# Layer 3's opening made within layer 2's last graphs, and three steps of layer 0 moved, in a four-layer graph attention kernel

## The reference

```python
h = jnp.maximum(_layernorm(x, axis=-1), 0.0)
x = x + L0(h, adj, ...)   # q, k, v; per 128-column chunk a softmax of clip(qk/sqrt(32), -10, 10), masked to -10
                          # ctx @ Wo.T + bo + h, layer norm, gamma, beta
x = x + L1(relu(ln(x)))   # e = leaky(e_i + e_j), softmax over neighbours, elu
x = x + L2(relu(ln(x)))   # the same with 8 heads, a prior, and @ W_out.T at the end
# layer 3
h1, h2, h3 = h @ W1, h @ W2, h @ W3
e = leaky_relu(h1 @ h2.T, 0.2)
e = where(adj > 0, e, -1e12)
x = x + relu(softmax(e) @ h3)
```

## Time and profile before

| | |
|---|---|
| median of 3 runs | 2028.11 us (2024.01 to 2032.48) |
| profiled execution | 2026.8 us, of which span 2024.6 |
| mean granted TensorE clock | 0.911 |
| busy in the span: PE, DVE, ACT, POOL | 82%, 79%, 66%, 6% |
| 0 to 660 us (layer 0 and the way to layer 1): PE, DVE, ACT | 543.5, 546.0, 404.9 us |
| 660 to 1643 us (layers 1 and 2) | 780.4, 814.7, 756.6 us |
| 1643 to 2024.6 us (layer 3) | 326.5, 243.2, 178.1 us |

### The profile page before, as it was taken

One profiled execution on the slowest core, in us unless ns is written; L12 is line 12 of the kernel. 1 busy time (PEld: TensorE's weight loads), 2 busy tenths in 40 slices (PEclk: granted clock), 3 DMA queues, 4 the chain that ended last, 5 costly groups with the idle time before them and its releaser, 6 DMA issues. The chain is left out here.

```text
span 2024.6 us, 36872 instructions
## 1 busy us (share of the span) xinstructions
PE 1650.5 (82%) x13620; PEld 1056.3 (52%) x13620; DVE 1603.9 (79%) x2710; ACT 1339.6 (66%) x1751; POOL 126.2 (6%) x130
## 2 busy tenths in 40 slices
PE   3998988988986577999999777977797748999997
PEld 1444443434433356777777556755675534555554
DVE  4888988988987557888888889898888747666764
ACT  2766666666663576777776989888888814554553
POOL 1000010010000100000000000000000000000000
PEclk7999999999998688999999878888888869999999
DMA  8634634635622311111111112111211120000000
GB/s 232 160 102 122 141 92 115 147 89 127 141 71 68 119 43 39 47 43 42 50 46 43 54 64 74 65 64 55 74 65 64 63 89 1 11 22 10 10 11 21
DMA packets 74922, 146.49 MB, mean 72 GB/s; under 512 B 11937, under 2 KB 34722, under 8 KB 74754
## 3 DMA queue, kind: packets, MB, share of 16 engines
q1 hardware_dynamic: 74754, 144.23, 25.4%
HBM read 101.85 MB, written 8.78 MB: 55 GB/s over the span
## 5 line engine op out<-in xcount | busy, mean ns | idle before, releaser
L1097 ACT ACTIVATE g<-s_all,steep_d 128x1024 fp8e4<-128x1024 f32 x608 | 642.3, 1135 | 40.6 <-DMA s_all<-s_rows 20.6
L1032 PE MATMUL acc<-parts,g 128*128 128x102 bf16 (+1 forms) x6144 | 417.2, 229 | 24.7 <-DVE sums L1188 24.5
L1032 PEld LDWEIGHTS acc<-parts,g 128*128 128x128 fp8e4 x6144 | 401.5, 100 | 57.4 <-issue 40.5
L1014 PE MATMUL post<-parts,edge 128*128 128x396 bf16 (+1 forms) x1024 | 233.7, 384 | 88.4 <-DVE base L1196 88.4
L583 ACT ACTIVATE e<-s_ps 128x1024 f32<-128x1024 f32 x256 | 248.1, 1022 | 24.5 <-PE s_ps L439 22.3
L1181 DVE TENSOR_TENSOR g<-g,edge 128x1024 int32<-128x1024 int32 x192 | 228.1, 1220 | 34.1 <-ACT g L1097 34.1
L732 DVE SCALAR_TENSOR_TENSOR e<-e,bound 128x1024 f32<-128x1024 f32 x160 | 191.0, 1228 | 43.4 <-ACT e L583 43.3
L1014 PEld LDWEIGHTS post<-parts,edge 128*128 128x128 fp8e4 x1024 | 102.5, 102 | 195.9 <-issue 111.5
L435 PE MATMUL s_ps<-qs,ks 128*128 128x512 f32 x512 | 193.5, 487 | 6.6 <-DMA ks<-split 4.9
L451 PE MATMUL sum_ps<-e,pick 128*32 128x256 f32 x2048 | 142.2, 396 | 67.6 <-DVE e L732 57.4
L1879 ACT ACTIVATE z<-z,shift 128x1024 f32<-128x1024 f32 x64 | 73.6, 1149 | 161.0 <-DVE shift L1955 161.0
(11 more groups left out here) (158 smaller groups left out, 2146.7 us busy)
## 6 DMA issues: line engine op xcount, KB each, us to landing
s_all<-s_rows SPq DMA_DIRECT2D x96, 512.0 KB, 3.7
inv_all<-inv_rows SPq DMA_DIRECT2D x256, 128.0 KB, 2.9
qs<-split SPq DMA_DIRECT2D x128, 128.0 KB, 3.2
ks<-split SPq DMA_DIRECT2D x128, 128.0 KB, 2.8
x<-in_x SPq DMA_DIRECT2D x8, 512.0 KB, 6.8
inv_rows<-inv SPq DMA_DIRECT2D x32, 128.0 KB, 1.8
adj_in<-in_adj SPq DMA_DIRECT2D x8, 512.0 KB, 4.1
out_x<-x SPq DMA_DIRECT2D x8, 512.0 KB, 3.2
```

What stands on the lines that cost most here:

```text
L1014: ins = pe.matmul(self.post[:, it % 2, 0:H * 3 * W1].rearrange("p (h k c) -> p h k c", h=H, k=3), self.c.edge[:, jt, it * P:(it + 1) * P], ...
L1032: ins = pe.matmul(self.acc[:, bank, o:o + self.NS], self.g[:, h % RING, jt, it * P:(it + 1) * P], self.upper[par][:, jt, h, :, :].rearrang ...
L1097: act.activation(self.g[:, h % RING, jt, :], self.s_all[:, h % 2, :], ACT.Relu, bias=self.steep_d[par][:, jt, h:h + 1], scale=STEEP, satur ...
```

## The change

Layer 3's `prepare` is taken out of its block and becomes the class `Opening`, whose parts are called from `additive_layers` for layer 2's last two graphs (and, in the branch that doesn't run, from a block of its own, `open_apart`). SyncE loads the three weights and `adj` tiles 0 to 3 between the heads of graph 6 and tiles 4 to 7 after heads 4 to 7 of graph 7; the input has four buffers instead of two. VectorE takes the statistics of graph 0 in step h=0 of graph 7, tiles 0 to 3 of `bias` in h=1 to 4, tiles 4 and 5 in h=6, tiles 6 and 7 in h=7. GpSimd's rstd stands in graph 7. PE makes `w12` in h=0, the transpositions in h=2 and the projection in h=4, in layer 2's `aux`. ScalarE copies `w12` and makes `h` in h=3, copies `ht` in h=6 and `q` in h=7. `bias`, the first `ht` and the first `q` lie in `c.arena`, which is also the `parts` buffer of the even graphs.

In layer 0 PE's `output(b - 1, 1)` goes from step 11 to 10, VectorE's second `residual` from 12 to 10 and its `low` for k from 10 to 9.

```diff
--- before.py
+++ after.py
@@ -509,7 +509,7 @@
                         elif i == 8:
                             pe.wait_ge(v_ready, n + 1)
                             k(n)
-                    if i == 11 and not first:
+                    if i == 10 and not first:
                         if more:
                             pe.wait_ge(k_split, n + 1)
                         output(b - 1, 1)
@@ -807,14 +807,14 @@
                     if not first:
                         if i == 2:
                             update(b - 1, 0)
-                        elif i == 12:
+                        elif i == 10:
                             residual(b - 1, 1 - par, 1, more)
                         elif i == 14:
                             update(b - 1, 1)
                     if more:
                         if i == 5:
                             low(n, q_hi, bq, q_split, k_lo_stacked)
-                        elif i == 10:
+                        elif i == 9:
                             low(n, k_hi, bk, k_split, q_lo_stacked)
                     if not (isinstance(b, int) and b >= B - 2):
                         if i == 4:
@@ -849,7 +849,7 @@
         sb = lambda name, shape, dt=F32: c.sb(name + "12", shape, dt, ctx)
         self.wh = sb("wh", [P, N])
         self.s_row = sb("s_row", [2 * HEADS[1], N])
-        self.parts = [sb(f"parts{i}_", [P, T * 8 * 3 * 2 * 17]) for i in range(2)]
+        self.parts = [c.arena, sb("parts1_", [P, T * 8 * 3 * 2 * 17])]
         self.s_all = sb("s_all", [P, 2, N])
         self.g = sb("g", [P, RING, T, N], F8)
         self.sums = [sb(f"sums{i}_", [P, T * 8 * 2 * 17]) for i in range(2)]
@@ -859,6 +859,107 @@
         self.acc = c.ps("acc12", [P, 4, HALF], ctx)
         self.post = c.ps("post12", [P, 2, HALF], ctx)
         self.aux = c.ps("aux12", [P, N], ctx)
+
+class Opening:
+
+    def __init__(self, c, w):
+        self.c, self.w = c, w
+        a = c.arena
+        self.bias = a[:, 0:T * HALF].bitcast(BF16).rearrange("p (t n) -> p t n", t=T)
+        self.ht, self.q = a[:, T * HALF:T * HALF + N], a[:, T * HALF + N:T * HALF + 2 * N]
+        self.w1_t, self.w2_t, self.w3 = (c.sb(k + "3", [P, F], F32)[:, :] for k in ("w1_t", "w2_t", "w3"))
...
+    def norm(self, aux):
...
+    def sp_adj(self, sp, adj_in, tiles):
+        for t in tiles:
+            if t >= 4:
+                sp.wait_ge(self.adj_used, t - 3)
+            sp.dma_start(adj_in[:, t % 4, :], self.w["adj"][t * P:(t + 1) * P, :]).then_inc(
+                self.adj_loaded[max(t // 2 - 1, 0)], 16)
+
+    def pe_w12(self, pe, aux):
+        pe.wait_ge(self.loaded, 48)
+        pe.matmul(aux[:, 0:F], self.w1_t, self.w2_t, start=True, stop=True).then_inc(self.w12_projected, 1)
+
+    def pe_turn(self, pe, aux):
+        pe.wait_ge(self.w12_ready, 1)
+        self.norm(aux).pe_turn(pe, 0, 0)
+
+    def pe_q(self, pe, aux):
+        nm = self.norm(aux)
+        pe.wait_ge(nm.h_t_ready, nm.upto(0))
+        project_rows(pe, aux, self.w12[:, :], self.ht).then_inc(self.q_projected, 1)
+
+    def act_w12(self, act, aux):
+        act.wait_ge(self.w12_projected, 1)
+        act.activation(self.w12[:, :], aux[:, 0:F], ACT.Copy).then_inc(self.w12_ready, 1)
+
+    def act_h_t(self, act, aux):
+        nm = self.norm(aux)
+        act.wait_ge(nm.h_turned, nm.upto(0))
+        act.activation(self.ht, aux[:, :], ACT.Copy).then_inc(nm.h_t_ready, 1)
+
+    def act_q(self, act, aux):
+        act.wait_ge(self.q_projected, 1)
+        act.activation(self.q, aux[:, :], ACT.Copy).then_inc(self.q_ready, 1)
+
+    def dve_stats(self, dve, aux):
+        nm = self.norm(aux)
+        nm.dve_stats(dve, 0)
+        nm.dve_moments(dve, 0)
+
+    def dve_bias(self, dve, adj_in, tiles):
+        for t in tiles:
+            dve.wait_ge(self.adj_loaded[max(t // 2 - 1, 0)], 64 if t < 4 else 32)
+            dve.tensor_scalar(self.bias[:, t, :], adj_in[:, t % 4, :], 0, NEG, ALU.is_le, ALU.mult).then_inc(self.adj_used, 1)
+
...
 class Additive:
@@ -1262,7 +1363,7 @@
     tail()
 
 
-def additive_layers(c, w1, w2):
+def additive_layers(c, w1, w2, third):
 
 
 
@@ -1276,6 +1377,8 @@
         one = Additive(c, ctx, 1, shared, w1, None)
         two = Additive(c, ctx, 2, shared, w2, one)
         both = (one, two)
+        adj_in3 = c.sb("adj_in3", [P, 4, N], I32, ctx)
+        aux = two.aux
         block = ctx.enter_context(nc.Block())
 
         def pieces(eng, slot, a, b, par, soon, later):
@@ -1302,6 +1405,13 @@
                     if at and a.H == 8 and h == a.H - 1:
                         at[0].sp_rows(sp, at[1], at[2])
                     a.sp_head(sp, b, par, h)
+                    if a is two and isinstance(b, int) and b == B - 2:
+                        if h == 0:
+                            third.sp_weights(sp)
+                        elif h % 2 == 1:
+                            third.sp_adj(sp, adj_in3, (h // 2,))
+                    elif a is two and isinstance(b, int) and b == B - 1 and h >= 4:
+                        third.sp_adj(sp, adj_in3, (h,))
                 if at and a.H == 4:
                     at[0].sp_rows(sp, at[1], at[2])
 
@@ -1320,6 +1430,8 @@
                 if at:
                     at[0].pool_rstd(pool, at[1])
                     at[0].pool_top(pool, at[1])
+                elif b == B - 1:
+                    third.norm(aux).pool_rstd(pool, 0)
 
             walk_both(pool, both, prepare, stage, lambda: None)
 
@@ -1360,6 +1472,13 @@
                     a.pe_head(pe, b, par, h, range(MID, T))
                     pieces(pe, 2 * h + 2, a, b, par, none, table)
                     a.pe_bases(pe, b, par, bases_at[a.H].get(2 * h + 2, ()))
+                    if a is two and isinstance(b, int) and b == B - 1:
+                        if h == 0:
+                            third.pe_w12(pe, aux)
+                        elif h == 2:
+                            third.pe_turn(pe, aux)
+                        elif h == 4:
+                            third.pe_q(pe, aux)
                     if before and before[0] is two:
                         if h == 4:
                             pe.wait_ge(two.base_ready, T * (b + 1))
@@ -1401,6 +1520,14 @@
                     pieces(act, 2 * h + 1, a, b, par, soon, later)
                     a.act_head(act, b, par, h, range(a.SC // 2, a.SC))
                     pieces(act, 2 * h + 2, a, b, par, soon, later)
+                    if a is two and isinstance(b, int) and b == B - 1:
+                        if h == 3:
+                            third.act_w12(act, aux)
+                            third.norm(aux).act_h(act, 0, 0)
+                        elif h == 6:
+                            third.act_h_t(act, aux)
+                        elif h == 7:
+                            third.act_q(act, aux)
                     if before and before[0] is one and h == 3:
                         one.act_neg_exp(act, before[1])
                     elif before and before[0] is two and h == 7:
@@ -1458,6 +1585,13 @@
                     elif h == 4:
                         a.dve_base(dve, b, (6, 7))
                     pieces(dve, 2 * h + 2, a, b, par, soon, later)
+                    if a is two and isinstance(b, int) and b == B - 1:
+                        if h == 0:
+                            third.dve_stats(dve, aux)
+                        elif h < 5:
+                            third.dve_bias(dve, adj_in3, (h - 1,))
+                        elif h > 5:
+                            third.dve_bias(dve, adj_in3, (2 * h - 8, 2 * h - 7))
                     if h == 2:
                         a.dve_base(dve, b, (2, 3))
                     if before and h == 1:
@@ -1693,17 +1827,14 @@
-def layer3(c, x_out, adj, w):
+def layer3(c, x_out, opening):
...
+        bias, w3, w12 = opening.bias, opening.w3, opening.w12
+        q = [opening.q, sb("q3_1", [P, N])[:, :]]
+        ht = [opening.ht, sb("ht3_1", [P, N])[:, :]]
...
         @block.sync
         def _(sp):
-            for dst, name in ((w1_t, "w1_t"), (w2_t, "w2_t"), (w3, "w3")):
-                sp.dma_start(dst[:, :], w[name]).then_inc(loaded, 16)
-            for t in range(T):
-                if t >= 2:
-                    sp.wait_ge(adj_used, t - 1)
-                sp.dma_start(adj_in[:, t % 2, :], adj[t * P:(t + 1) * P, :]).then_inc(adj_loaded[t % 2], 16)
...
-            walk(pool, lambda n, par: nm.pool_rstd(pool, n), stage)
+            walk(pool, lambda n, par: None, stage)
...
-            pe.wait_ge(loaded, 48)
-            pe.matmul(o_ps[:, 0:F], w1_t[:, :], w2_t[:, :], start=True, stop=True).then_inc(w12_projected, 1)
...
-            walk(pe, prepare, stage, tail)
+            walk(pe, lambda n, par: None, stage, tail)
...
-            walk(act, prepare, stage, tail)
+            walk(act, lambda n, par: None, stage, tail)
...
-                stats(n, par)
-                for t in range(T):
-                    dve.wait_ge(adj_loaded[t % 2], 16 * (t // 2 + 1))
```

(47 more changed lines are left out.)

26 lines of the change are left out of this document (13 added, 13 removed).

## The result

The changed kernel takes **2004.53 us** (median of 4 runs, 2001.29 to 2006.04), the kernel before, run beside it, 2027.53: a ratio of **0.9883, 95% interval 0.9858 to 0.9907**. That is 23 us less, where the forecast had 8.8 (2018.0 against 2026.8); the time lies half a us inside the lower end of the range (2004 to 2027), between rivals A and B. The profiled execution took 2006.04 us with 2004.2 of span, the one before 2026.8 with 2024.6 of span.

A forecast was written before the change was run, and what follows sets the result against it. It saw a serial chain at layer 3's start, PE and VectorE alternating in layer 2's last graph, and PE in layer 0 with one stall per graph. 2026.8 - 11.6 (opening: -17.1 + 5.5) + 2.8 (layer 0) = 2018.0 us; range 2004 to 2027.

The forecast's parts named there:

- A: Layer 0: PE's clock holds through the new gap, -5 in all, total 2010 us; chance 0.22.
- B: Layer 0: the stall goes altogether, VectorE not waiting for the output; 3.0 a graph, 21 in all, 1994 us; chance 0.07.
- The opening's gain: Start of layer 3: first masking at +7.8 instead of +25.4 us, 17.6 less; gain 17.1 after 0.5 taken off.
- The opening's cost in layer 2: Layer 2's last graph: work added on VectorE and PE makes it end 5.5 us later, bounds 4.2 and 9.2.
- the 0.6 by which VectorE was to end later than PE: End of layer 2's last graph: VectorE 5.5 us behind in all, PE alone 4.9, the later one ending the layer.
- The walk through the queues: Layer 0, one graph step by step: VectorE waits 2.3 us for the output product, PE stalls 3.7 at step 11.
- The second stall: Layer 0, before step 13: PE's stall short, about 1.5 us, leaving PE warm.
- the term of +0.4 us a graph: Layer 0: PE cold at step 11, output product at 491.3 against 490.91; +2.8 over seven graphs, bounds -5 and +14.
- C: Layer 0: PE falls to the lower level at steps 11 and 13 of every graph, +2.0 each, 2029 us; chance 0.10.
- D: Opening: PE enters layer 3 late (+3.8) or graph 7's costs reach their bound (+3.7), 2022 us with either; chance 0.19.
- E: Layer 3's entry: another engine's entry ends after the scores, early work unused; price and chance within D's.
- the forecast's own signs of being wrong: Residual finds its product ready, layer 0's period changes over 1 us, or PE's first scores begin over 5 us after layer 2.

The follow-up runs named there:

- e5_residual_11: The changed kernel with layer 0's second residual in step 11 instead of 10: 1977.77 us, ratio 0.9782 to the kernel before.
- e7_both: The changed kernel with the second residual at step 11, and mask tiles 4 to 7, projection and copy of q moved to layer 2's end: 1977.21 us, ratio 0.977.
- e2_opening_only: The changed kernel with layer 0 as before, so only layer 3's opening is made early: 2011.64 us, ratio 0.9922 to the kernel before.
- e9_opening_again: The same program as e2_opening_only, timed again on another chip: 2011.36 us, ratio 0.9925 to the kernel before.

## Why the prediction was wrong, step by step

**The opening's gain was right.** Forecast: first masking at +7.8 instead of +25.4, 17.6 less. Measured: it starts 8.23 after the update's end, and the stretch went from 26.59 to 9.45, 17.1 less. In the eight traces with the new opening it is 8.97 to 9.70, in the six others, where the old one stands, 26.3 to 28.4. PE's entry, for which there was no row, was taken as VectorE's 4.01 and is 4.25 (3.91 to 4.50 in the eight traces); the slow first scores were taken as 3.75 and are 3.78. The Trainium skill, "Runtime: NRT & Kernel Launch", section "Instruction fetch mechanics", has a taken branch to code outside the fetched pages stall the engine for a fetch. The trace agrees in kind: before the change PE's idle time there ended with the landing of the weights, now it is put down to issue and nothing else. No row shows the fetch itself.

**The opening's cost in layer 2 was sized too high:** 5.5 forecast, 3.4 measured. The six traces with the added work inside the heads have 119.6 to 119.8 us for this stretch, the six with the old opening 114.8 to 116.4, so 3.9 by the means. By its terms: VectorE reaches the combine of graph 6 8.79 us after the sums of head 0 (1567.28 to 1576.07). The same two rows of VectorE's timeline in the kernel before are 7.22 apart, so it is 1.6 later where 1.9 was forecast:

```profile
1575.66 1.07 DVE L1188 TENSOR_REDUCE sums<-acc 128x136 f32<-128x408 f32 x2
...
1582.88 1.28 DVE L1205 TENSOR_TENSOR sums<-base,sums 128x1088 f32<-128x1088 f32 x1
```
From PE's second base pair to the last update it is 50.7, before 47.7 (1641.61 less 1593.88): 3.0, PE's two added pieces, as forecast (2.5 by the means of six and six traces). Of the forecast's terms the last one failed, the 0.6 by which VectorE was to end later than PE: its last sums find PE's products just made. These pieces make 4.6. The stretch grew by only 3.4 because its part ahead of VectorE's first added instruction is 1.2 shorter in this pair (49.2 against 50.4); over all fourteen traces that part is 49.0 to 50.4 with either opening, so the 1.2 is scatter.

**Layer 0 is the step that failed.** The walk through the queues was right to 0.1 us in the graph shown: the wait of 2.28 (2.05 to 2.96 over the seven graphs), the stall of 3.81 (3.67 to 3.81 in five, 3.25 and 3.26 in the last two), the clips beside GpSimd. The second stall, forecast as 1.5, is 1.61 in the one graph where the clock held and 0.28 to 1.07 in the six where it fell, since PE's slower work fills it. What failed is the term of +0.4 us a graph, the price of the clock. The forecast took one graph for each of its two numbers.

*After the change* it had PE at the lower level from the sums of step 11 on, in each graph, 13.2 us from there to the next output product (478.1 to 491.3), or 12.1 with the clock up. The seven graphs have 12.92, 12.15, 12.15, 12.65, 13.02, 12.06 and 12.05. Where the sums take 1.94 it is 12.9 to 13.0, the forecast to 0.2; where they take 1.07, in four of seven, it is 12.05 to 12.15, rival A's figure, although the values and scores behind these sums are slow in three of the four. What slows down there is not on the path: the inversion hangs on the sums, and what the scores lose comes out of the 1.5 us that PE would have waited for the clips of step 13. The mean is 12.4, 0.8 less than forecast.

*Before* it had 5.5 us from the sums of step 13 to the output product, read from one graph. The seven have 6.52, 5.53, 5.54, 6.57, 5.53, 6.35 and 5.40, a mean of 5.9: the low clock cost 0.4 more than I took, and there every us of it is on the path, since PE has nothing to wait for until the output product.

Together 0.4 - 0.8 - 0.4 = -0.8 a graph. Both means hold in the other traces: 5.9 in each of the five with the old layer 0, 12.2 to 12.5 in the four with the moves. The graph's period fell by 0.47 in this pair (525.45 to 522.18 us over seven), and another 0.7 us went ahead of the first of them, where PE's wait for clips is 0.69 (at 96.95) instead of 1.88 (at 97.62). The 0.3 a graph between -0.8 and -0.47, 2.3 us in all, were lost again elsewhere. One place is seen on PE in the changed kernel, slow sums after a short wait where the kernel before had fast ones (1.07 after the same 2.10):

```profile
511.06 1.94 PE L451 MATMUL sum_ps<-e,pick 128*32 128x256 f32 x16 [2.10 <-DVE e L732]
```

The rest is not assigned. It is partly scatter: by the means of those five and four traces the seven graphs are 4.7 us shorter, 0.67 a graph.

Windows over the seven graphs, in the kernel before, the changed one and `e5_residual_11`, in the columns of the windows above:

```profile
109.68:635.13 525.45, 461.88 (x3736) 217.68 (x3735) 460.87 (x641) 343.90 (x465) 49.19 (x43) 0.96 0.46 112
```

```profile
109.02:631.20 522.18, 460.77 (x3735) 218.02 (x3735) 459.17 (x641) 343.29 (x465) 52.57 (x43) 0.97 0.47 113
```

```profile
109.29:604.01 494.72, 445.86 (x3735) 213.43 (x3735) 456.91 (x642) 344.26 (x465) 40.59 (x43) 1.00 0.50 120
```

The change takes 1.1 us of slow matmuls and 2.2 us of idle time (length less PE's busy time, 63.6 to 61.4) out of 525. With the residual at step 11 PE's busy time is 16.0 less than in the kernel before, at a granted clock of 1.00, the higher level (2.4 GHz), and its idle time 14.7 less. Half of that gain is clock.

**The rivals.** A (the clock holds, 2010) has the time of four graphs in seven, in three of them for a reason that it didn't name: the clock fell there too, but where it costs nothing. B, "VectorE does not wait for the output", is not what the change does. `e5_residual_11` takes that wait away, by a later residual and not by an earlier product as B had it, and its layer 0 is 31 us shorter than that of the kernel before (671.19 to 640.05), where B had 21. C (cold twice, 2029) didn't occur: the second gap, 0.28 to 1.61, was never followed by slow sums. D's late entry (+3.8) is excluded by the 4.25, its bound of the cost by the 3.4. E too: the early work is used.

**The sum of the error.** 20.4 us less in the trace against 8.8 forecast: 11.6, of which 6.8 in layer 0, 2.1 the opening's cost, 3.2 the stretch that isn't edited, and 0.5 the other way. The 6.8 are 8.4 for the clock, mis-sized on both sides (7 times 1.2), and 0.7 ahead of the seven graphs, less the 2.3 lost again. Had layer 0 been priced by means over its seven graphs (-0.8 each instead of +0.4) the forecast would have been 2009.6. The range held the time by half a us only; nothing in it stood for the 5 us by which a stretch without edits differs between two traces. Of the forecast's own signs of being wrong none appeared: the residual waits, PE starts before 5 us, and the mean period changed by less than 1 us (single graphs by -1.8 to +1.1). They tested the walk and the entry, not the price of the clock.

## What to carry to other kernels

When a product and the work that reads it are moved in two in-order queues, walk both queues and try one step of the consumer's other work between them. In this kernel, directly behind the product the consumer waits, two steps later its work piles up in front of the next hand-over, and the one step in between was worth as much as the whole change. Price a lowered clock by where the slow instructions stand, on the path or ahead of a wait, and over all repetitions of the loop, not from one. Before a difference of a few us is explained, compare stretches that nobody edited.

## What the runs showed of the hardware that was not expected

- A PE stall of nearly the same length is followed by different speeds: 3.81 by sums of 1.07 and 3.67 by sums of 1.94, in the same trace, at the same place of two graphs. In the kernel before, stalls of 4.26 to 4.33 are followed by sums of 1.36 to 1.94. Which graphs have slow sums changes from trace to trace of the same layer 0. A wait of 2.10 is followed by sums of 1.07 in one kernel and of 1.94 in the other. With the residual at step 11, where no wait is longer than 2.5, the granted clock is 1.00 over 495 us in `e5_residual_11` and in `e7_both`, but even there one such wait has slow sums behind it, in `e7_both`:

```profile
204.09 1.94 PE L451 MATMUL sum_ps<-e,pick 128*32 128x256 f32 x16 [2.47 <-DVE e L732]
```

- The clock can fall a us after a stall as well as in it: sums at 1.07 and a granted clock of 1.00, values behind them at 1.62, scores at 2.07 and a granted clock of 0.50.
- The same program differs by 5 us (856.1 and 850.7) over one stretch of 850 between two executions (`e2_opening_only` and `e9_opening_again`), and a single graph of it by 3.5 (66.9 and 63.4).
